# Attention scores on row tiles of TensorE: four full, four half-row and four one-row products per head instead of eight full ones

## The reference

```python
a = _layer_norm(audio_kv, ln_gamma, ln_beta)
Q = (hidden_states @ Wq.T).reshape(B, Tt, HEADS, HEAD_DIM).transpose(0, 2, 1, 3)
K = (a @ Wk.T).reshape(B, Ta, HEADS, HEAD_DIM).transpose(0, 2, 1, 3)
V = (a @ Wv.T).reshape(B, Ta, HEADS, HEAD_DIM).transpose(0, 2, 1, 3)
scores = jnp.einsum('bhtd,bhsd->bhts', Q, K) * scale
scores = jnp.where(mask, scores, jnp.float32(-jnp.inf))
attn = jax.nn.softmax(scores, axis=-1)
out = jnp.einsum('bhts,bhsd->bhtd', attn, V).transpose(0, 2, 1, 3).reshape(B, Tt, D)
return hidden_states + jnp.tanh(gate) * (out @ Wo.T)
```

## Time and profile before

| what | value |
|---|---|
| median of 3 runs | 1995.74 us (1995.33 to 1997.52) |
| the profiled execution, its own time | 2000.36 us |
| its span, first to last instruction | 1998.2 us |
| TensorE matmul busy | 1958.0 us, 98% of the span, 8720 instructions |
| TensorE weight loads busy (they overlap matmuls) | 1589.9 us, 80% |
| VectorE busy | 1613.8 us, 81% |
| GpSimd busy | 1462.7 us, 73% |
| ScalarE busy | 1344.3 us, 67% |
| mean granted TensorE clock | 0.994 |

### The profile page before, as it was taken

The page is one execution under the profiler, slowest core; times in us unless marked ns, Lnnn a source line. Parts: engine busy times, 40 slices in busy tenths (PEclk is TensorE's granted clock), DMA queues, the critical chain, the costliest instruction groups (busy, mean ns, idle before and its releaser), DMA issues.

```text
span 1998.2 us, 26443 instructions
## 1 busy us (share of the span) xinstructions
PE 1958.0 (98%) x8720; PEld 1589.9 (80%) x8720; DVE 1613.8 (81%) x2082; ACT 1344.3 (67%) x2434; POOL 1462.7 (73%) x806
## 2 busy tenths in 40 slices
PE   6899999999999999999999999999999999999997
PEld 5787778888788887888888888888888888888886
DVE  7688768887788877888788887888878888778877
ACT  5768876578756686657865678665876568756554
POOL 4899996668865778666876669767697667966664
PEclk8999999999999999999999999999999999999999
DMA  7577544554355443554445543455433644435422
GB/s 264 174 252 242 189 172 167 220 180 140 130 194 188 168 170 112 212 197 142 151 149 194 191 168 119 163 197 182 175 129 130 253 151 150 154 124 191 164 93 106
DMA packets 136502, 341.96 MB, mean 171 GB/s; under 512 B 55856, under 2 KB 56880, under 8 KB 135472
## 3 DMA queue, kind: packets, MB, share of 16 engines
q1 hardware_dynamic: 136368, 340.28, 48.9%
HBM read 288.86 MB, written 51.36 MB: 170 GB/s over the span
## 4 chain that ended last, share of the span: by engine, by line
PE 79%; POOL 8%; ACT 6%; DVE 4%; issue 1%; DMA 1%; SPq 0%; ACTq 0%; DVEq 0%; POOLq 0%
PE pj L445 14%; PE pj L449 14%; PE pj L447 14%; PE sc L398 5%; PE sc L402 5%; PE sc L399 5%; PE sc L372 5%; PE sc L373 5%; PE pv L392 5%; PE pv L393 5%; POOL a_lo L1138 4%; DVE mq L821 2%; POOL p_lo L1104 2%; PE pj L381 1%; ACT prob L619 1%
## 5 line engine op out<-in xcount | busy, mean ns | idle before, releaser
L1104 POOL TENSOR_TENSOR p_lo<-prob,p_hi 128x1024 fp32r<-128x1024 f32 x255 | 611.4, 2408 | 188.1 <-ACT p_hi L624 188.1
L445 PE MATMUL pj<-a_hi,w_hi 128*128 128x512 f32 x1024 | 404.2, 395 | 7.7 <-DVE v_st L865 3.0
L449 PE MATMUL pj<-a_hi,w_lo 128*128 128x512 f32 x1024 | 401.3, 392 | 0.0
L447 PE MATMUL pj<-a_lo,w_hi 128*128 128x512 f32 x1024 | 401.0, 392 | 0.0
L821 DVE TRANSPOSE_TENSOR_REDUCE mq<-sc 128x32 f32<-128x1024 f32 x256 | 304.0, 1225 | 79.9 <-PE sc L373 79.1
L888 DVE SCALAR_TENSOR_TENSOR xy<-sc,tg_b,xy 128x1024 f32<-128x1024 f32 x244 | 306.2, 1273 | 31.6 <-PE sc L402 25.6
L619 ACT ACTIVATE prob<-prob 128x1024 f32<-128x1024 f32 x256 | 271.4, 1060 | 89.2 <-DVE prob L843 88.8
L843 DVE TENSOR_TENSOR prob<-sc,m_b 128x1024 f32<-128x1024 f32 x256 | 301.6, 1220 | 4.4
L1108 POOL TENSOR_TENSOR prob<-prob 128x1024 f32<-128x1024 f32 x126 | 302.1, 2398 | 0.0
L1115 POOL TENSOR_TENSOR r_b<-o,r_b 128x512 f32<-128x512 f32 x62 | 81.2, 1310 | 267.9 <-DVE r_b L860 267.9
L624 ACT CAST p_hi<-prob 128x1024 fp32r<-128x1024 f32 x256 | 269.5, 1053 | 3.5
(11 more groups left out here) (129 smaller groups left out, 3731.6 us busy)
## 6 DMA issues: line engine op xcount, KB each, us to landing
w_hi<-kept_hi SPq DMA_DIRECT2D x225, 512.0 KB, 3.7
w_lo<-kept_lo SPq DMA_DIRECT2D x225, 512.0 KB, 4.6
xy<-in_xT SPq DMA_DIRECT2D x32, 512.0 KB, 6.6
cx<-in_ctx SPq DMA_DIRECT2D x32, 512.0 KB, 7.4
kept_hi<-w_hi SPq DMA_DIRECT2D x32, 512.0 KB, 5.3
kept_lo<-w_lo SPq DMA_DIRECT2D x32, 512.0 KB, 6.0
out_y<-xy SPq DMA_DIRECT2D x7, 2048.0 KB, 9.8
w_raw<-in_wq SPq DMA_DIRECT2D x8, 512.0 KB, 5.1
```

Source lines behind the costliest of these rows:

```text
L445: pe.matmul(dst, w_hi[:, w, cols], s_hi[:, i], start=i == 0, stop=False)
L447: pe.matmul(dst, w_hi[:, w, cols], s_lo[:, i], start=False, stop=False)
L449: mm = pe.matmul(dst, w_lo[:, w, cols], s_hi[:, i], start=False, stop=i == KT - 1)
L1104: pool.tensor_tensor(p_lo[:, 2 * i:2 * i + 2], prob[:, h, 2 * i:2 * i + 2], f32(p_hi[:, 2 * i:2 * i + 2]), ALU.subtract).then_inc(pl_done, 1)
```

## The change

It does three things.

1. **Scores.** `kt[:, h, 0]` is as before. `qt` now holds Q hi in the other half of both of its slots, Q hi in the own half of slot 0 and Q lo in the own half of slot 1; `kt[:, h, 1]` holds K hi in the *other* half and a constant 1.0 in the own half. Banks 0 and 2 get one full product with `qt[:, h, 0]` (hi·hi + lo·hi) and lack hi·lo; banks 1 and 3 get one with `qt[:, h, 1]` (hi·lo + lo·hi) and lack hi·hi. The missing part is a product of 64 rows, in the own half of the partitions for banks 0 and 2 and in the other half for banks 1 and 3, so that two neighbours stand in different row halves of the array. The mask comes from four products of one row each, at partitions 0, 32, 64 and 96 (`m_row`), one per bank. The order is four full, four one-row, four half-row products. `s_done` is counted after the second and the fourth half-row product, where before it was counted after the fourth and the eighth full one.
2. **Around them.** ScalarE copies Q hi three times per head instead of twice. The mask takes four small ScalarE instructions per batch instead of two. `FILL` moves two projection steps per head from behind the output step to before it. The scores of a head wait for both `subtract` of the head before at once, instead of one after the other.
3. **Weights and tail.** (WO, 7) is split two bodies later, at the end of GpSimd's body 8 and the start of ScalarE's body 9, into its own slot, and written to HBM in body 9. In `last_body` GpSimd makes both blocks of the last `p_low`, VectorE none, and TensorE does the second half of `values` before the last `out_pair`.

```diff
-BODY_SPLITS += [[(WV, PAIRS - 1), (WO, PAIRS - 1), (WO, PAIRS - 3)], [(WO, PAIRS - 2)]]
+BODY_SPLITS += [[(WV, PAIRS - 1), (WO, PAIRS - 3)], [(WO, PAIRS - 2)], [(WO, PAIRS - 1)]]
...
-FILL = ((5, 4, 7, 2, 18), (5, 4, 9, 2, 16))
+FILL = ((5, 4, 9, 2, 16), (5, 4, 11, 2, 14))
...
         def out_split(k):
 
-            b, j = divmod(k - 1, PAIRS)
-            return b, WO, j - 1
...
+            return (0, WO, k - 2) if 2 <= k < PAIRS + 2 else (1, WO, 0)
...
                 ge(pe, acc_done, k * 4 - (6 if h and kind != "last" else 8))
-                for i in range(2):
-                    ge(pe, sub_done, k * 4 + 2 * h + i - 1)
-                    for s in (2 * i, 2 * i + 1):
-                        cols = slice(s * P, (s + 1) * P)
-                        pe.matmul(sc[:, s], kt[:, h, 0, cols], qt[:, h, 0], start=True, stop=False)
-                        mm = pe.matmul(sc[:, s], kt[:, h, 1, cols], qt[:, h, 1], start=False, stop=True)
+                ge(pe, sub_done, k * 4 + 2 * h)
+                own, other = halves[h], halves[1 - h]
+                tiles = [slice(s * P, (s + 1) * P) for s in range(TB)]
+                for s in range(TB):
+                    pe.matmul(sc[:, s], kt[:, h, 0, tiles[s]], qt[:, h, s % 2], start=True, stop=False)
+                for g in range(TB):
+                    row = slice(32 * g, 32 * g + 1)
+                    pe.matmul(sc[:, g], m_row[row], kt[row, g // 2, 1], start=False, stop=False)
+                for s in (0, 2):
+                    pe.matmul(sc[:, s], kt[own, h, 0, tiles[s]], qt[own, h, 1], start=False, stop=True)
+                    mm = pe.matmul(sc[:, s + 1], kt[other, h, 1, tiles[s + 1]], qt[other, h, 0], start=False, stop=True)
                     mm.then_inc(s_done, 1)
...
                 act.copy(qt[half, h, 0], pj[1][half]).then_inc(qh_done, 1)
-                act.copy(qt[other, h, 0], pj[1][half]).then_inc(qh_done, 1)
+                for slot in range(2):
+                    act.copy(qt[other, h, slot], pj[1][half]).then_inc(qh_done, 1)
...
                 act.copy(kt[half, h, 0], pj[0][half]).then_inc(kh_done, 1)
-                act.copy(kt[half, h, 1], pj[0][half]).then_inc(kh_done, 1)
+                act.copy(kt[other, h, 1], pj[0][half]).then_inc(kh_done, 1)
...
-                    split_w(b, WO, PAIRS - 1, WQ)
                     for i in range(3, KT):
                         x_low(b, i, (b + 1) % 2)
...
                 pe.wait_ge(oadd_done, k * 2 + 1)
                 key_sums(1, 0, pv[0][:, 0])
+                values(k, 1, 1)
+                key_sums(1, 1, pv[0][:, 0])
                 pe.wait_ge(acc_done, 4 * k - 6)
                 out_pair(k - 2, 3, lower, done=False)
-                pe.wait_ge(plv_done, 1)
-                values(k, 1, 1)
-                key_sums(1, 1, pv[0][:, 0])
...
-                dve.wait_ge(ph_done, k * 4 + 4)
-                dve.tensor_tensor(p_lo[:, 3], prob[:, 1, 3], f32(p_hi[:, 3]), ALU.subtract).then_inc(plv_done, 1)
```

More of the change, by code:

```diff
@@ L71, in xattn_kernel @@
         kt, qt = sb("kt", [P, 2, 2, T], F32R), sb("qt", [P, 2, 2, T], F32R)
+        m_row = sb("m_row", [P, P], F32R)
         vt = sb("vt", [P, T])
@@ L300, in batch @@
                     k = b * PAIRS + j
+                    if k == PAIRS:
+                        m = NUMBER[WO, PAIRS - 1]
+                        sp.dma_start(w_raw[:, m % 2], wts[WO][PAIRS - 1]).then_inc(w_ld[m % 2], 16)
+                        keep_split(m - 1)
+                    if k == PAIRS + 1:
+                        keep_split(NUMBER[WO, PAIRS - 1])
                     load_kept(WV, (j + 1) % PAIRS, k)
@@ L586, in _, with split_w @@
         def _(act):
-            def split_w(b, kind, pair, slot=None):
+            def split_w(b, kind, pair):
                 if not splits(b, kind, pair):
@@ L590, in split_w @@
                 m = NUMBER[kind, pair]
-                slot = kind if slot is None else slot
                 act.wait_ge(w_ld[m % 2], 16 * (m // 2 + 1))
-                ge(act, w_out[slot], 32 * PAIRS if slot != kind else 32 * pair)
-                act.copy(w_hi[:, slot], w_raw[:, m % 2]).then_inc(whi_done, 1)
+                ge(act, w_out[kind], 32 * pair)
+                act.copy(w_hi[:, kind], w_raw[:, m % 2]).then_inc(whi_done, 1)
             def gather_maxima(k, h):
@@ L635, in k_high @@
                 ge(act, s_done, k * 4 + 4)
-                half = halves[h]
+                half, other = halves[h], halves[1 - h]
                 act.copy(kt[half, h, 0], pj[0][half]).then_inc(kh_done, 1)
-                act.copy(kt[half, h, 1], pj[0][half]).then_inc(kh_done, 1)
+                act.copy(kt[other, h, 1], pj[0][half]).then_inc(kh_done, 1)
             def o_move(k, h):
@@ L662, in mask_rows @@
                 act.nop(nofuse=True)
-                for h, row in ((0, HD), (1, 0)):
-                    act.activation(kt[row:row + 1, h, 1], mask_u8[row:row + 1], ACT.Identity, bias=masked[row:row + 1],
+                for g in range(TB):
+                    row = slice(32 * g, 32 * g + 1)
+                    act.activation(m_row[row], mask_u8[row, g * P:(g + 1) * P], ACT.Identity, bias=masked[row],
                                    scale=-MASKED).then_inc(mrow_done, 1)
@@ L1054, in _ @@
             dve.memset(eps[:], EPS).then_inc(eps_done, 1)
-            dve.memset(m_b[:], 0.0).then_inc(row_done, 1)
-            dve.memset(r_b[:], 0.0).then_inc(row_done, 1)
-            dve.wait_ge(row_done, 2)
-            dve.memset(r_b[HD:HD + 1], 1.0).then_inc(row_done, 1)
-            dve.memset(r_b[0:1], 1.0).then_inc(row_done, 1)
-            dve.wait_ge(row_done, 4)
-            for h in range(2):
-                dve.tensor_copy(kt[halves[1 - h], h, 1], m_b[halves[1 - h]]).then_inc(init_done, 1)
-                dve.tensor_copy(qt[halves[1 - h], h, 1], r_b[halves[1 - h]]).then_inc(init_done, 1)
+            dve.memset(r_b[:], 1.0).then_inc(row_done, 1)
+            dve.wait_ge(row_done, 1)
+            for h, half in enumerate(halves):
+                dve.tensor_copy(kt[half, h, 1], r_b[half]).then_inc(init_done, 1)
             for i in FIRST_BY_V:
@@ L1076, in _ @@
             dve.wait_ge(mask_ld, 16)
-            dve.wait_ge(init_done, 5)
-            for h, row in ((0, HD), (1, 0)):
-                dve.tensor_scalar(kt[row:row + 1, h, 1], mask_u8[row:row + 1], -MASKED, MASKED, ALU.mult,
+            for g in range(TB):
+                row = slice(32 * g, 32 * g + 1)
+                dve.tensor_scalar(m_row[row], mask_u8[row, g * P:(g + 1) * P], -MASKED, MASKED, ALU.mult,
                                   ALU.add).then_inc(mrow_done, 1)
@@ L1177, in last_body @@
                 pool.tensor_copy(ones, one_from).then_inc(ones_done, 1)
-                p_low(k, 0, 0)
-                p_low(k, 0, 1)
-                p_low(k, 1, 0)
-                pool.wait_ge(ph_done, k * 4 + 4)
-                pool.tensor_tensor(p_lo[:, 2], prob[:, 1, 2], f32(p_hi[:, 2]), ALU.subtract).then_inc(pl_done, 1)
+                for h in range(2):
+                    for i in range(2):
+                        p_low(k, h, i)
             pool.memset(ident[:], 0.0).then_inc(ident_done, 1)
```

60 lines of the change are left out of this document (27 added, 33 removed).

## The result

The changed kernel has a median of 2053.09 us (2052.68 to 2056.26, 4 runs) against 1995.53 for the kernel before: a ratio of 1.0287, 95% interval 1.0275 to 1.0300. The forecast was 2019, +23 us, with a range of 1988 to 2070. The result is +57.6 us: the right direction, inside the range, and two and a half times the size.

What follows compares the result with a forecast made beforehand. TensorE's nearly gapless list was taken as the bound. Per head -0.226 + 0.33 + 0.09 = +0.195, x 126 = +24.6; with -2.4 and +1 once, +23 us on 1995.7 gives 2019 us, range 1988 to 2070.

Steps and rivals of the forecast that it cites:

- Bound and cover: Ordinary pairs: TensorE's list is nearly gapless, each product moves the end by 0.226 us; other engines' added work is covered.
- Score products, -0.226: Scores, per head: eight full products become four full, four one-row, four half-row, taking seven products' time, -0.226 us.
- Changes of shape, +0.33: TensorE's scores: three changes per head at 0.11 us of open load each, +0.33; bounds 0 to 0.27 per change.
- My price for that case: Rival, pipe empties at each change of shape: 0.16 tail plus 0.11 load, 0.27 us each; 2068 us, chance 0.20.
- The wait at the output step, +0.09: Output step, per head: `subtract` comes 0.67 us later, the step only 0.56, so +0.09 us on average after slack.
- free changes: Rival, scores: changes of shape cost nothing, but nearly all the gain becomes a wait for `subtract`; 1991 us, chance 0.25.
- Weight split: GpSimd, pair 6 of the first batch: the split taken out lands where time is free, -2.4 us once.
- VectorE's and GpSimd's block in the last pair: Last pair: TensorE does the last `values` during its former VectorE wait, GpSimd's block grows; about -1 us once.
- the forecast case: Scores: a change of shape costs 0.03 to 0.2 us; twelve products take about 1.9 to 2.0 us; chance 0.33.
- Loads one after the other: Rival, scores: small products' loads go 0.11 us apart, +0.09 per head; about 2005 us, chance 0.14.
- products not side by side: Rival, scores: small products each take full time, twelve for eight, +0.90 us per head; 2108 us, chance 0.08.
- The third Q copy: ScalarE, per head: the extra copy costs 0.58 us but is covered, since VectorE's chain moves 0.67 later.

Runs made afterwards that it cites:

- e2: The changed kernel with its four one-row mask products issued twice in a row, no change of shape added: 2078.87 us.
- e4: The changed kernel with the `FILL` numbers of the kernel before, so the output step comes two products earlier: 2096.72 us.
- e6: The kernel before with the last output weights split two bodies later and the new order of the last pair, scores and `FILL` unchanged: 1992.50 us.
- e1: The changed kernel without its four one-row mask products, leaving two changes of shape per head instead of three: 2006.28 us.
- e5: The changed kernel with its half-row products reordered: own half on banks 0 and 2, then other half on banks 1 and 3: 2076.58 us.
- e7: The kernel before with one one-row product added per head between the fifth and sixth full score product: 2068.15 us.
- e8: The kernel before with only the last output weights split two bodies later: 1993.47 us.

## Why the prediction was wrong in size

**Bound and cover: right.** An ordinary pair stayed a gapless list of TensorE, and what was added to it arrived at the end: pairs 8 to 62 took 1663.8 us before and 1712.8 after, +49.0 for 110 heads, 0.445 each. (That is their mean; the last pair of a batch grew by 1.2 us, the others by 0.8 to 0.9.)

**Score products, -0.226: right.** Four one-row products share one product's time, four half-row ones two; e2 shows it for the first, the pairs of starts at 1043.04 for the second.

**Changes of shape, +0.33: the step that failed.** I took the open load, 0.11, and assumed the pipe need not empty. It measured 0.21 each, +0.63, so the term was 0.30 short, 38 us over 126 heads. The bounds, 0 to 0.27, held it. The rule I had weighed against it (the Trainium skill, "TensorEngine Tiling (Array Packing)", Key Properties: a change of tiling mode drains TensorE) agrees with the trace in kind: behind a full product and behind a half-row one the next shape's load starts only 0.32 us after that product's start. The trace does not show TensorE quite empty by then, since that product's record lasts 0.39 us, with a modelled end; why the load waits 0.10 beyond the product's 0.226 stays open. My price for that case, 0.16 for the tail of a product's record, was too high. Weighing the two ends by the nearest row alone, and not by the fact that a page named the mechanism of the upper one, put the forecast in the wrong half of its own range.

**The wait at the output step, +0.09: right in form, and gone.** By the prediction's own formula, 0.226 - c - 0.025 per head, the wait ends where a change costs c = 0.20. At 0.21 nothing is left. The timeline after, at the output step of the same head:

```profile
1048.78 2.36 DVE L851 TENSOR_TENSOR prob<-sc,m_b 128x1024 f32<-128x1024 f32 x2
...
1050.03 0.40 PE L458 MATMUL pj<-x_hi,w_lo 128*128 128x512 f32 x1
...
1050.06 0.19 PEld L407 LDWEIGHTS sc<-o_hi,w_hi 128*128 128x128 f32 x1
1050.26 0.40 PE L407 MATMUL sc<-o_hi,w_hi 128*128 128x512 f32 x1
```

The load comes 0.03 us after the product ahead of it, which hides it. e4 shows the mechanism at full size, and the rule behind the "free changes" rival with it: by it, had the changes cost nothing, most of the gain would have become this wait. That rival itself, 1991, was not run.

**What I left out: +0.04 per head.** After the last change of a head the next few full products stand 0.23 to 0.24 apart instead of 0.226, as they do after the transposes before. The 0.04, 5 us in all, is what is left of 0.445. Read directly, from the first product after the scores to the next head's scores, ordinary pairs take 0.16 us more in head 0 and 0.12 in head 1 than before, 0.11 of it open load, so that 0.01 to 0.05 is left.

So per head -0.226 + 0.63 + 0.04 = 0.444, against 0.445 measured.

**The one-off terms: near.** Weight split -1.8 in its place, forecast -2.4; VectorE's and GpSimd's block in the last pair -1.5 by e6, forecast -1. From the last pair's first scores to the end the changed kernel takes 45.9 us instead of 44.0: +1.9, forecast +1. The scores' part of that is then +3.4, not +2. Sum: 126 x 0.445 = 56.1, -1.8 and +1.9 give +56.2 of the +57.6. The 0.445 is carried over to the first batch here; its own piece, from the first scores to those of pair 8, grew by 3.4 us, 2 less than that, and what hides them isn't shown.

**The signs named ahead.** The mask starts lie together and loads lie open three times per head, as forecast. The block is 2.10 us, over the 1.9 to 2.0 of the forecast case, which told of the dearer change. The output step waits in 58 places and not in most heads. Pair 6 of the first batch is not 2.4 us shorter: the split's gain came mostly in pair 7.

**The other rivals.** Loads one after the other and products not side by side are refuted by e2. The figure of the Trainium skill's "TensorE: Matmul & The Clock Gate", Part 3 (3.07x for four tiles) gives, as an estimate, 1.30 products for a mask round. The trace differs: the second round of e2 made the block 0.23 us longer, one product's time. The third Q copy was covered: in the waits, ScalarE waits 194.5 us for VectorE's group maxima after, behind those copies among others, and 144.3 before, so the copies were done in time.

## What to carry to other kernels

Count the changes of tile shape in TensorE's list, not only the products: each cost 0.21 us here, about one full 512-column product, so packing pays only where it saves more products than it has changes. Without the masks (e1) it saved two with two changes, and an ordinary pair took what it took before. A group of small products wants to be long and of one shape; two groups, of one and of two rounds, inside a stream of full products lose. Before shortening a producer, look at when it releases its first result: here the release moved later although the work of the list got less, and only the padding ahead of the consumer hid that (e4).

## What the runs showed that I had not expected

- Half-row products in different row halves start independently of each other: one started 0.33 us before a product that stands ahead of it in the list (e5). Its semaphore still came in the order of the list, so a release that stands behind a product that starts later comes late: by 0.22 us here.
- A one-row product in a full stream costs 0.64 us, 2.8 times a full one (e7).
- The stretch ahead of the first scores, the same code in e8 as in the kernel before, took 38.9 us in one profiled execution and 42.3 in the other. The spans of single executions carry a few us of that, so pieces of the timeline were compared above rather than spans. What sets it stays open.
